# Output product ahead of the router's in a second attention, and 71 expert tiles in place of 72

## The reference, cut to what matters

```python
# layer 0: 8 experts, each token goes to 2 of them
x = x + moe0(layernorm(x))          # silu(x_e @ w1) * (x_e @ w3) @ w2, sorted by expert
# layer 1: attention over a context of 77 rows, one head of 256
xn = layernorm(x)
attn = softmax(queries(xn) @ keys.T / 16)
x = x + (xn + attn @ values) @ Wo.T + bo
# layer 1: 32 experts, each token goes to 4; logits = layernorm(x) @ router_w.T + bias
x = x + moe1(layernorm(x))
```

## Time and profile before

| | |
|---|---|
| median of three runs | 1439.91 us (1436.26 to 1440.08) |
| profiled execution | 1447.97 us |
| its span, first to last instruction | 1446.1 us |
| PE busy | 1322.6 us, 91% of the span |
| ACT, DVE, POOL busy | 594.8, 766.0, 663.6 us |
| first experts in the trace | 419 to 801 us |
| second attention in the trace | 805 to 940 us |

### The profile page before, as it was taken

The page is one execution under the profiler, slowest core; times in us unless marked ns, Lnnn a source line. Parts: engine busy times, 40 slices in busy tenths (PEclk is TensorE's granted clock), DMA queues, the critical chain, the costliest instruction groups (busy, mean ns, idle before and its releaser), DMA issues. The chain is left out here.

```text
span 1446.1 us, 29159 instructions
## 1 busy us (share of the span) xinstructions
PE 1322.6 (91%) x7743; PEld 1056.2 (73%) x7744; DVE 766.0 (53%) x1965; ACT 594.8 (41%) x1314; POOL 663.6 (46%) x905
## 2 busy tenths in 40 slices
PE   7998999999879999999999599847999999989993
PEld 4665777777558888888888387724888888858882
DVE  4884888887732222222222488693233333347764
ACT  2455777777322222222222377635333333322110
POOL 1213565665113333333332366504555555257775
PEclk9998999999889999999999599966999999999997
DMA  2108322222731111111111677554455555745554
GB/s 96 59 30 307 114 92 89 78 96 100 288 119 48 50 50 51 50 50 51 51 51 37 202 228 218 163 232 155 154 164 161 162 161 156 131 125 161 161 161 126
DMA packets 117387, 179.94 MB, mean 124 GB/s; under 512 B 17210, under 2 KB 91979, under 8 KB 113996
## 3 DMA queue, kind: packets, MB, share of 16 engines
q1 hardware_dynamic: 80980, 100.29, 20.8%
q0 software_dynamic: 20736, 56.65, 14.6%
q10 hardware_dynamic: 15608, 22.25, 4.3%
HBM read 115.13 MB, written 59.77 MB: 121 GB/s over the span
## 5 line engine op out<-in xcount | busy, mean ns | idle before, releaser
L1228 POOL DMA_INDIRECT xg<-t_xn,token x160 | 151.7, 948 | 157.7 <-PE psum L2093 72.8
L2167 POOL DMA_INDIRECT su_yg<-t_y,slot x128 | 125.4, 980 | 67.9 <-issue 38.1
L2105 PE MATMUL psum<-gu,m_xT 128*128 x640 | 154.2, 384 | 0.0
L1465 PE MATMUL psum<-w,m_hT 128*128 x576 | 136.3, 380 | 0.8 <-ACT m_hT L1384 0.8
L1403 DVE TENSOR_TENSOR m_h<-psum,m_h 128x512 f32<-128x512 f32 x72 | 49.8, 691 | 164.8 <-ACT m_h L1378 164.8
L2105 PEld LDWEIGHTS psum<-gu,m_xT 128*128 128x128 f32 x640 | 117.2, 193 | 13.2
L1444 PE MATMUL psum<-w,m_xT_high 128*128 x288 | 120.8, 420 | 0.0
L2064 DVE TENSOR_TENSOR m_h<-psum,m_sg 128x256 f32<-128x256 f32 x80 | 34.0, 425 | 162.0 <-ACT m_sg L2043 161.9
L1444 PE MATMUL psum<-w,m_xT_low 128*128 x288 | 114.9, 399 | 0.0
L1444 PE MATMUL psum<-w_low,m_xT_high 128*128 x288 | 114.2, 396 | 0.0
L1465 PEld LDWEIGHTS psum<-w,m_hT 128*128 128x128 f32 x576 | 103.8, 190 | 12.4 <-issue 1.2
(11 more groups left out here) (305 smaller groups left out, 3126.1 us busy)
## 6 DMA issues: line engine op xcount, KB each, us to landing
t_y<-m_y SPq DMA_DIRECT2D x80, 256.0 KB, 2.2
w<-in_w SPq DMA_DIRECT2D x8, 1024.0 KB, 11.3
t_x<-at_x SPq DMA_DIRECT2D x64, 128.0 KB, 2.1
t_w_low<-at_low ACTq DMA_DIRECT2D x64, 128.0 KB, 1.7
w_low<-t_w_low SPq DMA_DIRECT2D x8, 1024.0 KB, 13.3
at_yg<-t_y SPq DMA_DIRECT2D x32, 256.0 KB, 3.1
gu<-in_gu ACTq DMA_DIRECT2D x8, 1024.0 KB, 11.9
w<-in_x SPq DMA_DIRECT2D x16, 256.0 KB, 2.8
```

What stands on the lines that cost most here:

```text
L1228: pool.indirect_dma_start(out=g.xg1[j % GB][:, k * D:(k + 1) * D], out_offset=None, in_=g.xn4, in_offset=bass.IndirectOffsetOnAxis(ap=g.to ...
L1465: last = pe.matmul(ps_y[:, 0:D], hT[:, c * P:(c + 1) * P], g.w2[:, bass.ds(ex * (MC * D) + c * D, D)], start=(c == 0), stop=(c == MC - 1))
L2105: last = pe.matmul(ps_gu[p][:, k * 2 * M1:(k + 1) * 2 * M1], xT[p][:, at:at + P], g.gu[:, bass.ds(ex[k] * (DC * 2 * M1) + c * 2 * M1, 2 * ...
L2167: pool.indirect_dma_start(out=yg[p][k][:, :], out_offset=None, in_=g.y1, in_offset=bass.IndirectOffsetOnAxis(ap=g.slot[:, at:at + 1], axis ...
```

## The change

`NS0` becomes 71. The loops over tiles end at a multiple of their body, and the tiles left over are written out behind them; the wait for the scattered rows counts 36 and 35 scatters on the two semaphores instead of 36 and 36.

In the second attention PE's step becomes S, XN, WO, XM, R, PT. ACT copies in the order `at_xnT`, `at_xn` (normalise), `at_xmT`, `at_lg`, `at_prT`. SP stores `at_xm` first, then `at_x`, then `at_xmT` of the tile before, and loads last.

```diff
-NS0 = NTOK * K0 // P + E0
+NS0 = NTOK * K0 // P + E0 - 1
 # sync engine, one step
-                if (t := stage(s, 0)) is not None and not (t.loop is None and t.off < GB):
-                    load(t)
+                if (t := stage(s, XM + 1)) is not None:
+                    p = t.mod(2)
+                    sp.wait_ge(xm_done, t.n + 1)
+                    sp.dma_start(g.xn4[rows(t), :], xm[p][:, :]).then_inc(xm_st[p], 16)
                 if (t := stage(s, WO + 1)) is not None:
                     q = t.mod(4)
                     sp.wait_ge(x3_done, t.n + 1)
                     sp.dma_start(g.x3[rows(t), :], x3[q][:, :]).then_inc(x3_st[q], 16)
-                if (t := stage(s, XM + 1)) is not None:
-                    p = t.mod(2)
-                    sp.wait_ge(xm_done, t.n + 1)
-                    sp.dma_start(g.xn4[rows(t), :], xm[p][:, :]).then_inc(xm_st[p], 16)
+                if (t := stage(s, XM + 2)) is not None:
+                    p = t.mod(2)
                     sp.wait_ge(xm_out, t.n + 1)
                     sp.dma_start(g.xn4T[:, :].rearrange("p (c n) -> p c n", c=DC)[:, :, rows(t)],
                                  xmT[p][:, :].rearrange("p (c n) -> p c n", c=DC)).then_inc(xmT_st[p], 16)
+                if (t := stage(s, 0)) is not None and not (t.loop is None and t.off < GB):
+                    load(t)
```

More of the change, by code:

```diff
@@ L1384, in step @@
                     act.activation(hT[:, :], ps_ht[:, 0:M0], ACT.Copy).then_inc(h_out, 1)
-            steps(act, 4, NS0, NS0 + 2, 2, step)
+            steps(act, 4, NS0 - NS0 % 2, NS0 + 2, 2, step)
         @block.vector
@@ L1410, in step @@
                     dve.tensor_copy(y[p][:, :], ps_y[:, 0:D]).then_inc(y_out, 1)
-            steps(dve, 6, NS0, NS0 + 3, 2, step)
+            steps(dve, 6, NS0 - NS0 % 2, NS0 + 3, 2, step)
         @block.tensor
@@ L1468, in step @@
                     last.then_inc(y_mm, 1)
-            steps(pe, 8, NS0, NS0 + 3, GB, step)
+            steps(pe, 8, NS0 - NS0 % GB, NS0 + 3, GB, step)
 def attention1_phase(nc, g):
@@ L1539, in load @@
                     for p in range(2):
-                        sp.wait_ge(g.s_y0[p], NS0 // 2 * 16)
+                        sp.wait_ge(g.s_y0[p], (NS0 + 1 - p) // 2 * 16)
                 sp.dma_start(yg[t.mod(GB)][:, :].rearrange("p (k n) -> p k n", k=K0),
@@ L1569, in step @@
                                  xmT[p][:, :].rearrange("p (c n) -> p c n", c=DC)).then_inc(xmT_st[p], 16)
-            steps(sp, FIRST, NT, NT + XM + 2, BODY, step)
+                if (t := stage(s, 0)) is not None and not (t.loop is None and t.off < GB):
+                    load(t)
+            steps(sp, FIRST, NT, NT + XM + 3, BODY, step)
             for st in x3_st:
@@ L1694, in step @@
                     act.activation(xnT[t.mod(4)][:, :], ps_x[t.mod(2)][:, 0:D], ACT.Copy).then_inc(x_out, 1)
-                if (t := stage(s, R)) is not None:
-                    p = t.mod(2)
-                    act.wait_ge(r_mm, t.n + 1)
-                    wait(act, ix_done, t.shift(-1).n)
-                    act.activation(lg[p][:, :], logits_of(t), ACT.Copy).then_inc(lg_done, 1)
+                if (t := stage(s, XA)) is not None:
+                    wait(act, x_t, t.shift(-1).n)
+                    lna.apply_scalar(act, x2[t.mod(8)][:, :], xn[t.mod(2)][:, :], t).then_inc(xn_done, 1)
                 if (t := stage(s, XM)) is not None:
@@ L1707, in step @@
                     act.activation(xmT[p][:, :], ps_m[:, 0:D], ACT.Copy).then_inc(xm_out, 1)
-                if (t := stage(s, XA)) is not None:
-                    wait(act, x_t, t.shift(-1).n)
-                    lna.apply_scalar(act, x2[t.mod(8)][:, :], xn[t.mod(2)][:, :], t).then_inc(xn_done, 1)
+                if (t := stage(s, R)) is not None:
+                    p = t.mod(2)
+                    act.wait_ge(r_mm, t.n + 1)
+                    wait(act, ix_done, t.shift(-1).n)
+                    act.activation(lg[p][:, :], logits_of(t), ACT.Copy).then_inc(lg_done, 1)
                 if (t := stage(s, PT)) is not None:
@@ L1738, in step @@
                     last.then_inc(s_mm, 1)
[L1739 to L1748, removed]
                 if (t := stage(s, XN)) is not None:
@@ L1756, in step @@
                     last.then_inc(x_t, 1)
[L1757 to L1764, removed]
                 if (t := stage(s, WO)) is not None:
@@ L1778, in step @@
                         .then_inc(wo_mm, 1)
+                if (t := stage(s, XM)) is not None:
+                    p = t.mod(2)
+                    pe.wait_ge(xm_done, t.n + 1)
+                    wait(pe, xm_out, t.n)
+                    for c in range(DC):
+                        last = pe.transpose(ps_m[:, c * P:(c + 1) * P], xm[p][:, c * P:(c + 1) * P], g.ident[:, :])
+                    last.then_inc(xm_t, 1)
+                if (t := stage(s, R)) is not None:
+                    p = t.mod(2)
+                    pe.wait_ge(xm_out, t.n + 1)
+                    pe.wait_ge(exp_done, NT if t.loop is None and t.off + 5 > NT else t.shift(5).n)
+                    pe.matmul(logits_of(t), ones3[:, :], bias3[:, NB * LK:NB * LK + E1], start=True, stop=False)
+                    for c in range(DC):
+                        last = pe.matmul(logits_of(t), xmT[p][:, c * P:(c + 1) * P], wr[:, c * E1:(c + 1) * E1],
+                                         start=False, stop=(c == DC - 1))
+                    last.then_inc(r_mm, 1)
                 if (t := stage(s, PT)) is not None:
```

## The result

The changed kernel takes 1450.88 us (median of 4 runs, 1446.34 to 1452.83), the kernel before on the same chip 1439.97. The ratio is 1.0069, 95% interval 1.0044 to 1.0095. A second measurement of the same kernel gave 1.0088, 1.0054 to 1.0122. It is slower by 0.7 to 0.9%, 10 to 13 us; by the medians 10.9 and, in the second, 10.0 us. The forecast, 1438.6 us with a range up to 1443.5, was wrong, and in its sign: -1.3 us was expected.

The account below looks back on a forecast made before the run. PE was taken as the bound, busy 91% of the span. The terms -5.2 - 4.8 + 9.9 - 1.2 = -1.3 us took 1439.9 to 1438.6 us, with an 8-in-10 range of 1432.5 to 1443.5.

Parts of the forecast that it names:

- Part 1: First experts: one tile fewer takes a whole tile of PE work away, -5.18 us.
- Part 2: Second attention: SP storing `at_xm` first removes ACT's waits for that store, -4.8 us, bounds 0 and -4.83.
- I carry the difference over unchanged: Whole kernel: the profiled execution's 8 us above the median of the runs is kept, giving 1439.9 - 1.3 us.
- Part 3: Second attention, PE: scores wait for ACT's copy of the logits, 0.35 us in 26 steps, +9.1 us.
- Part 4: Second attention: load and `at_xmT` store rings through SP take 6.9 to 7.3 us per two steps; +9.9 with Part 3.
- I take 3.68 a step: Second attention: step of 3.68 us in place of 3.30, +9.9 us for Part 3 and Part 4 together.
- Part 5: End of the second attention: output product ahead of router and transposes brings the last tile earlier, -1.2 us, bounds 0 and -2.
- (b): Second attention: the `at_xmT` ring decides with late landings, 3.9 us a step, sum +6.2, 1446 us; chance 0.11.
- the median landing is 2.3: Second attention: argument against (b), with a slower step loading the DMA less.
- (c): Second attention: the load ring decides, `at_yg` landing in 3.5 us or more, +1.8, 1441.7 us; chance 0.12.
- (a): Second attention: logits stall smaller than the removed waits, 1435.2 us, or 1428.7 with no stall; chance 0.26.
- (d): First router's tables: the odd width of 71 columns costs 3 us or more, 1441.6 to 1443 us; chance 0.03.

Follow-up runs that it names:

- f1: Kernel before with only the 71 tiles, second attention unchanged; 1433.4 us, ratio 0.9947.
- f4: Kernel before with only PE's and ACT's new orders, SP's old order, 72 tiles; 1444.9 us, ratio 1.0033.
- g4: Changed kernel with SP's step reordered to load, `at_xm` store, `at_xmT` store, output tile last; 1439.0 us, ratio 0.9974.
- g6: f1 with the output tile's store moved to the end of SP's step; 1432.2 us, ratio 0.9948 to the kernel before.
- g5: g4 with PE's router product ahead of the `at_xm` transposes and ACT's `at_lg` copy ahead of `at_xmT`; 1432.4 us, ratio 0.9948 to the kernel before.
- the last execution: Profiled execution of the changed kernel, unchanged, in its second measurement; 1444.74 us.
- the first execution: Profiled execution of the changed kernel in its first measurement; 1446.34 us.
- g3_load_early: Changed kernel with SP's load first in its step again, `at_xmT` store still behind the output tile; 1448.6 us, ratio 1.0031.
- g2_xmT_early: Changed kernel with SP's `at_xmT` store moved ahead of the wait for the output tile, load still last; 1441.8 us, ratio 0.9982.

## Why the prediction was wrong, step by step

The size and the sign both failed. By the medians the tile gave 6.5 us (f1), the new order of PE and ACT cost 5.0 (f4) and SP's new order 11 to 12 (g4 to the changed kernel); that adds up to a loss of 9 to 10 where 10 to 11 was measured. The forecast had -1.3.

**Part 1, the tile:** right, 5.0 us by the traces for 5.18. The times of f1_tiles71 would have it larger.

**Part 2, the removed waits:** the wait went as said. Its price was mis-sized: -4.8 us was read in an execution 8 us above the median. In the kernel before run again it is -1.8, in f1's profile -6.7, and g6 against f1 shows none in the medians. The step that failed is "I carry the difference over unchanged": the difference lay, by 3.1 us, in the very term that the change was to remove, and 4.3 and 3.5 us of it in the fill and behind the phase. The two profiled executions, 1447.97 and 1446.34 us, would even look like the forecast's -1.3 us. That is chance: the one lay 8 us above the median of its kernel, the other 4.5 below.

**Part 3, the logits' wait:** right. Idle times of 0.18 and 0.34 us take turns where 0.35 was forecast; the pitch without a wait for a DMA is 3.62 against g6's 3.30, 25 x 0.31 = 7.8 us for 9.1. Between g4 and g5 it is 6.6 us by the medians, and 0.26%, 3.7 us, by the ratios, with intervals that allow 0 to 9. Its name in the view was wrong: "issue" for the most part.

**Part 4, the two rings:** this is the step that failed. "I take 3.68 a step" gave the rings only what they add to the logits' wait, 0.8 us. Measured, from g4 to the changed kernel, it is 11 to 12 us by the medians, and 6.3 us of this stretch even in the shortest executions (96.75 - 90.43). The length of the ring was right (7.0 to 7.3 us for two steps forecast, 7.2 measured). Wrong was to use it with the median landing, 2.3 us, though the earlier trace rows show 3.9 as the longest. A ring as long as two steps cannot make up a late landing in the next step. And the sum left out the price of the clock: a landing 2.2 us late became 3.2 us.

**Part 5, the drain:** not seen. It is 18.4 us after, 17.7 and 17.9 before, 0 within 1 us for the -1.2 forecast. In f4_pe_act_only, with SP's old order, it is 16.5, which is the shortening forecast; that SP's order undoes it is likely but not shown.

**The rivals:** (b) was the mechanism, with the `at_xmT` ring in first place, a pitch of 3.9 and a fall of the clock; it had 0.11, and its 1446 us was still 5 us short, since it too gave back the 4.8 of Part 2. The evidence against it, "the median landing is 2.3", was the same error. (c), the load ring, is real and small, 1 to 3 us. (a) and (d) were wrong.

## What to carry to other kernels

When a change makes a store or a load wait for an event later in the step, work out the loop from that event through the landing back to it, and compare it with the step. Where they are as close as here, 7.2 us both, price it by the spread of the landings, each late one in full, with the clock on top where the stall lowers it, and not by the median. A wait in the list is not yet a loss: compare the same step with one where the wait is absent. And before a removed wait is booked as a gain, look how far its execution lies from the median of the runs: what lies above the median may be that wait. Here SP's in-order queue was cheapest with the item whose wait ends last at the end of the step (g4 and g6), and g6 with the old order of PE had the steadiest profile of all.

## What the hardware showed beyond that

- The clock does not follow the length of the last wait alone. PE waited 1.73 us (833.84, the last execution) and 2.16 us (885.35, the first), and the granted clock behind it was 0.50 and 0.66, the lower level for all or part of the time; the steps then took 4.7 to 6.2 us for 3.54. But behind the 1.64 us at 865.34 in the first execution it stayed at 1.00, behind the 1.04 us at 850.62 in g3_load_early it was 0.51, and in g2_xmT_early it fell to 0.50 at 834 us (above) with no wait of PE longer than 0.45 us in the 10 us before. In g4_both_early, with PE idle 0.18 to 0.34 us in most steps, it was 1.00 from 824 to 925 us. What decides is not shown. The rows of the first execution and of g3_load_early (timeline of PE, and the window behind it, for each):

```profile
865.34 0.19 PE L1736 MATMUL psum<-at_bias,at_ones 3*128 x1 [1.64 <-issue]
```

```profile
868.00:872.00 4.00, 3.66 (x25) 3.03 (x25) 3.61 (x15) 3.06 (x10) 2.21 (x6) 1.00 0.62 189
```

```profile
850.62 0.19 PE L1736 MATMUL psum<-at_bias,at_ones 3*128 3x77 bf16 x1 [1.04 <-issue]
```

```profile
851.00:853.00 2.00, 2.00 (x9) 1.82 (x9) 1.31 (x7) 1.47 (x6) 0.83 (x2) 0.51 0.86 260
```

- Executions of one kernel spread more where a transfer is waited for. Of twelve each, measured together, g4_both_early (no such wait) had 1436.5 to 1442.3 us, g2_xmT_early 1437.2 to 1445.2, g3_load_early 1443.1 to 1455.5, and the kernel before 1436.7 to 1449.7.
